# Moving the normalising and adding of most batches behind the last tiles, the last root to ScalarE, and the writes behind the last load

## The chip, the core and the metric

The kernel runs on one core of one Trainium2 chip. Its time is the device time of one execution in microseconds (us), the median of several.

## What is computed

Input x is 8 batches of 512 tokens with 128 features, float32. Two residual blocks follow one another; each adds the layer norm of its branch to x.

```
x = x + layernorm(attn(layernorm(x)))
x = x + layernorm(ffn(layernorm(x)))
attn: inp = mix*x + (1-mix)*shifted x;  h = relu(inp @ W_in.T + b_in)
      state = state*decay + h  along the sequence;  states @ W_out.T + b_out
ffn:  top-2 of 8 experts per token, softmax over the two gate logits
      y = silu(x @ w0[e]) * (x @ w1[e]) @ wo[e];  out = sum over the two of weight * y
```

The change touches only the last step: the sum of a token's two expert rows, its layer norm, and the addition to x.

## The kernel before

Everything is written out by engine, with semaphores. The 4096 tokens give 8192 (token, expert) pairs, which are sorted by expert into 71 tiles of 128 rows (TILES). After a preamble all engines walk through slots t = 0 to 75 (`slots()`). In slot t the engines work on several tiles at once: TensorE turns tile t (L1514), multiplies tile t-1 by w0 and w1 in three parts each (L1519 to L1521), turns the gated tile t-2 (L1554), and multiplies tile t-3 by wo (L1570). ScalarE takes the upper part of tile t (L586), scales the finished rows y of tile t-4 (L606, `take_y`), computes silu of t-1 (L591) and copies the turned tile t-2 (L596). VectorE computes the lower part x_lo of tile t (L1214, for which TensorE waits before the next slot) and the product silu times l2 of tile t-1 (L1221), and every fourth slot the rows' numbers and weights (L1233 to L1247). POOL sends y of tile t-4 with an indirect DMA to `pair_rows` in DRAM (L422, `send_y`).

Tiles are ordered so that the pairs of batches 0 to 5 are complete after tile 55 (FIRST_OLD_TILES = 56), those of batch 6 after tile 62 (OLD_TILES = 63) and those of batch 7 after the last. SP loads the pairs of a group of batches back to SBUF as soon as the y of those tiles have landed (`load_pairs`, L345; GROUPS are batches 0-1, 2-3, 4-5, 6 and 7). The loads of the first three groups are 1 MB each, the last two 0.5 MB.

For each batch of 4 x 128 tokens then follow, in this order: the sum of the two rows of a token (VectorE, L1252), statistics (VectorE, L1258) and their aggregate (L1264), 1/sqrt(variance + eps) by group (POOL, an add L443 and a power L447, `one_over_sd`), the offset -mean/sd by group (VectorE, L1270, `offset`), the normalising of four 128-column pieces (ScalarE, L624, `normalise4`), the addition to x (`add_normed`: POOL L454 for batches 0 and 1, VectorE L1284 for 2 to 6) and the write of the group (SP, L350, 0.5 MB for two batches). These pieces are placed by hand in the slots FIRST_OLD_TILES + 6 to + 18, behind the tile's own work of each engine, by the `if t == ...` tables of L469 to L480 (POOL), L686 to L699 (ScalarE) and L1371 to L1413 (VectorE). Since every engine works in order, a piece that waits holds up the tile work behind it.

Batch 7 comes after the slots: load, sum, statistics, aggregate, root and offset, then two of its four pieces are normalised by VectorE (L1278, L1288) and two by ScalarE (L632), added, and written with the last write. SP's queue at the end reads: load of batch 7, then the writes of groups 0 to 4, each after a wait.

Of the kernel before, what the change touches and what calls it, by code (L numbers as in the profile page):

```python
# [59 lines left out]
def sandwich_kernel(nc, x_in, w_in_in, b_in_in, w_out_in, b_out_in, decay_in, mix_in,  # L60
                    gate_in, w0_in, w1_in, wo_in, out):
    ctx = ExitStack()
    with ctx:
# [221 lines left out]
        def _(sp):  # L285
# [72 lines left out]
            load_pairs(3)  # L358
            wait_sent(TILES)
            load_pairs(4)  # L360
            sp.wait_ge(d["out"], 2)
            write_out(0)
            sp.wait_ge(d["out_end"], 2)
            write_out(1)
            sp.wait_ge(d["out_end"], 4)
            write_out(2)
            sp.wait_ge(d["out_end"], 5)
            write_out(3)
            sp.wait_ge(d["out_end"], 6)
# [4 lines left out]
        def _(pool):  # L374
# [77 lines left out]
            def add_normed(b):  # L452
                pool.wait_ge(d["normed"], b + 1)
                pool.tensor_tensor(x[:, b * G:(b + 1) * G], x[:, b * G:(b + 1) * G],  # L454
                                   half_of_pairs(b, 0), ALU.add).then_inc(d["out"], 1)

# [9 lines left out]
            for k, s, t in slots():  # L466
# [4 lines left out]
                elif t == FIRST_OLD_TILES + 11:  # L471
                    one_over_sd(1, *SD_GROUPS[1])
                elif t == FIRST_OLD_TILES + 12:
                    add_normed(0)
                elif t == FIRST_OLD_TILES + 13:
                    one_over_sd(2, *SD_GROUPS[2])
                elif t == FIRST_OLD_TILES + 14:
                    add_normed(1)
                elif t == FIRST_OLD_TILES + 16:
                    one_over_sd(3, *SD_GROUPS[3])  # L480

            one_over_sd(4, *SD_GROUPS[4])

        @block.scalar
        def _(act):
# [142 lines left out]

            def normalise_last():
# [47 lines left out]
            for k, s, t in slots():  # L677
# [8 lines left out]
                if t == FIRST_OLD_TILES + 10:  # L686
                    normalise4(0, 0, 0, G)
                elif t == FIRST_OLD_TILES + 11:
                    normalise4(0, 1, 0, G)
                elif t == FIRST_OLD_TILES + 12:  # L690
                    normalise4(1, 2, 0, G)
                elif t == FIRST_OLD_TILES + 13:
                    normalise4(1, 3, 0, G)
                elif t == FIRST_OLD_TILES + 14:
                    normalise4(2, 4, 0, G)
                elif t == FIRST_OLD_TILES + 15:
                    normalise4(2, 5, 0, G)
                elif t == FIRST_OLD_TILES + 17:
                    normalise4(3, 6, 0, G)  # L699

            normalise_last()

        @block.vector
        def _(dve):
# [576 lines left out]

            def add_normed(b):
                dve.wait_ge(d["normed"], b + 1)
                dve.tensor_tensor(x[:, b * G:(b + 1) * G], x[:, b * G:(b + 1) * G],  # L1284
                                  half_of_pairs(b, 0), ALU.add).then_inc(d["out_end"], 1)
# [75 lines left out]
            for k, s, t in slots():  # L1361
# [20 lines left out]
                elif t == FIRST_OLD_TILES + 9:  # L1382
                    aggregate(2)
                    sum_pairs(1, 3)
                    stats_of(3)
# [245 lines left out]
```

## Time and profile before

| | us |
|---|---|
| median of 3 runs (lowest, highest) | 312.19 (311.73, 312.6) |
| the profiled execution | 312.02 |
| its span (first to last instruction) | 310.2 |
| TensorE busy in the span | 253.0 (82%) |
| VectorE | 201.2 (65%) |
| ScalarE | 186.1 (60%) |
| POOL | 176.1 (57%) |

The profile is one execution. Its span leaves out 1.8 us of the execution's time. Times of rows count from the start of the span. An engine's rows may overlap by a fraction of an instruction, since the next one starts while the last elements of the one before are written; TensorE's ends are modelled. "SPq" and "POOLq" are the queues' own instructions. Matmul records are merged in rows of the timeline.

### The profile page before, as it was taken

To read this page: it belongs to the slowest core of one execution; us is meant where nothing else is said; L and a number is where in the kernel's file an instruction comes from. 1 tells how busy PE (TensorE), PEld (TensorE's weight loads), DVE (VectorE), ACT (ScalarE), POOL (GpSimd) and SP (SyncE) were. 2 spreads that over 40 slices of the span, in tenths; PEclk is the share of its full clock that TensorE was granted. 3 is DMA by queue.
4 is the path that set the end of the run, shared out by engine and by line. 5 is a ranking of instruction groups with operands and counts; after the bars stand their busy time and mean duration, and the time that the engine had idled before them with its cause. 6 is when DMAs were issued, how large, how long until landed. Compare 5 with 4: busy or idle time off the path is not lost.

```text
span 310.2 us, 6821 instructions
## 1 busy us (share of the span) xinstructions
PE 253.0 (82%) x1615; PEld 214.3 (69%) x1615; DVE 201.2 (65%) x917; ACT 186.1 (60%) x451; POOL 176.1 (57%) x197
## 2 busy tenths in 40 slices
PE   0558534469999999999999999999999999999300
PEld 0226321357988899888889888898898888878300
DVE  3787979865496568559666846785554336887512
ACT  3575455616576865856675675666666666699601
POOL 7029567267237756774874787777233333568511
PEclk9965555578999999999999999999999999999955
DMA  5999511131121122112112212432322139020056
GB/s 145 207 383 301 150 53 45 43 79 36 46 60 54 42 73 71 44 62 77 56 44 83 66 45 65 111 107 86 88 73 57 51 91 366 17 77 17 0 154 184
DMA packets 27971, 29.56 MB, mean 95 GB/s; under 512 B 4538, under 2 KB 21148, under 8 KB 27936
## 3 DMA queue, kind: packets, MB, share of 16 engines
q1 hardware_dynamic: 22672, 20.04, 22.3%
q0 software_dynamic: 4544, 8.97, 8.9%
q8 instruction: 16, 0.26, 0.4%
q10 hardware_dynamic: 720, 0.13, 0.3%
q14 instruction: 19, 0.16, 0.2%
HBM read 17.53 MB, written 12.05 MB: 95 GB/s over the span
## 4 chain that ended last, share of the span: by engine, by line
PE 70%; DVE 8%; POOL 6%; DMA 5%; ACT 4%; issue 4%; POOLq 0%; SPq 0%; DVEq 0%; ACTq 0%
PE bank L1570 18%; PE bank L1519 10%; PE bank L1520 10%; PE bank L1521 10%; PE bank L1554 9%; POOL expert_rows L411 3%; PE bank L1514 3%; PE bank L1471 2%; PE bank L1444 2%; PE bank L1455 2%; PE bank L1464 1%; DMA sb_early<-pair_rows 1%; POOL pair_rows L422 1%; DMA sb_x<-in_L_attn_x 1%; POOL sb_rs L447 1%
## 5 line engine op out<-in xcount | busy, mean ns | idle before, releaser
L422 POOL DMA_INDIRECT pair_rows<-sb_y_rows,sb_y_pair x71 | 71.2, 1003 | 59.8 <-ACT sb_y_rows L606 40.2
L411 POOL DMA_INDIRECT expert_rows<-sb_row,sb_place x64 | 63.9, 999 | 30.1 <-issue 17.6
L1570 PE MATMUL bank<-sb_w_raw,sb_gatedT 128*128 x568 | 75.0, 275 | 0.0
L1221 DVE TENSOR_TENSOR sb_w_raw<-bank,sb_w_raw 128x512 f32<-128x512 f32 x71 | 48.9, 689 | 31.5 <-PE bank L1521 20.7
L1570 PEld LDWEIGHTS bank<-sb_w_raw,sb_gatedT 128*128 128x128 f32 x568 | 69.0, 192 | 0.1
L1519 PE MATMUL bank<-sb_w_parts,sb_x_hi 128*128 x142 | 62.8, 442 | 0.3 <-DVE sb_x_lo L1214 0.3
L596 ACT ACTIVATE sb_gatedT<-bank 128x512 f32<-128x512 f32 x71 | 42.4, 597 | 32.6 <-PE bank L1554 32.4
L1520 PE MATMUL bank<-sb_w_parts,sb_x_lo 128*128 x142 | 56.7, 399 | 0.0
L1521 PE MATMUL bank<-sb_w_parts,sb_x_hi 128*128 x142 | 56.5, 398 | 0.0
L591 ACT ACTIVATE sb_w_raw<-bank 128x512 f32<-128x512 f32 x71 | 42.5, 599 | 7.4 <-PE bank L1521 6.4
L1554 PE MATMUL bank<-sb_ident,sb_w_raw 128*128 128x128 f32 x284 | 42.9, 273 | 1.1 <-DVE sb_w_raw L1221 1.1
L1214 DVE TENSOR_TENSOR sb_x_lo<-bank,sb_x_hi 128x128 fp32r<-128x128 f32 x71 | 20.4, 287 | 34.8 <-ACT sb_x_hi L586 34.4
L1554 PEld LDWEIGHTS bank<-sb_ident,sb_w_raw 128*128 128x128 f32 x284 | 34.5, 140 | 10.4 <-issue 1.3
L586 ACT ACTIVATE sb_x_hi<-bank 128x128 fp32r<-128x128 f32 x71 | 19.6, 276 | 36.4 <-PE bank L1514 36.4
L1521 PEld LDWEIGHTS bank<-sb_w_parts,sb_x_hi 128*128 128x128 f32 x142 | 27.1, 191 | 6.4
L1519 PEld LDWEIGHTS bank<-sb_w_parts,sb_x_hi 128*128 128x128 f32 x142 | 27.5, 194 | 5.1 <-issue 1.6
L1520 PEld LDWEIGHTS bank<-sb_w_parts,sb_x_lo 128*128 128x128 f32 x142 | 27.4, 193 | 3.1
L606 ACT ACTIVATE sb_y_rows<-bank,sb_y_weight 128x128 f32<-128x128 f32 x71 | 25.7, 362 | 0.3 <-PE bank L1570 0.3
L1514 PE MATMUL bank<-sb_ident,sb_taken_rows 128*128 128x128 f32 x71 | 20.1, 283 | 2.8 <-DMA sb_taken_rows<-expert_rows 2.0
L261 POOL TENSOR_TENSOR sb_w_parts<-sb_w_raw,sb_w_parts 128x512 fp32r<-128x512 f32 x8 | 10.9, 1394 | 14.1 <-ACT sb_w_parts L553 14.1
L540 ACT ACTIVATE sb_row<-sb_x,sb_nm,sb_rs 128x128 f32<-128x128 f32 x32 | 14.3, 487 | 5.2 <-DVE sb_nm L767 5.2
L1444 PE MATMUL bank<-sb_early,sb_w_inT 128*128 128x512 f32 x16 | 12.0, 845 | 4.6 <-DVE sb_early L804 4.6
(177 smaller groups left out, 348.5 us busy)
## 6 DMA issues: line engine op xcount, KB each, us to landing
sb_taken_rows<-expert_rows SPq DMA_DIRECT2D x71, 65.5 KB, 1.8
sb_w_raw<-in_L_ffn_w SPq DMA_DIRECT2D x2, 2048.0 KB, 14.1
sb_w_raw<-pair_rows SPq DMA_DIRECT2D x3, 1024.0 KB, 7.2
out_dram<-sb_x SPq DMA_DIRECT2D x3, 512.0 KB, 6.2
pair_rows<-sb_y_rows,sb_y_pair POOLq DMA_INDIRECT x71, 2.5
sb_x<-in_L_attn_x SPq DMA_DIRECT2D x4, 256.0 KB, 6.4
expert_rows<-sb_row,sb_place POOLq DMA_INDIRECT x64, 2.3
sb_early<-pair_rows SPq DMA_DIRECT2D x2, 512.0 KB, 3.8
```

What stands on the lines that cost most here:

```text
L411: pool.indirect_dma_start(expert_rows[:, :], bass.IndirectOffsetOnAxis(ap=place[b % ROWS][:, k, j:j + 1], axis=0), row[b % ROWS][:, j, :], ...
L422: pool.indirect_dma_start(pair_rows[:, :], bass.IndirectOffsetOnAxis(ap=y_pair[group % 2][:, t % PAIRS:t % PAIRS + 1], axis=0), y_rows[slo ...
L591: act.activation(silu[t % 2][:], p_l1[:], ACT.Silu).then_inc(c["silu"], 1)
L596: act.activation(gatedT[t % 2][:], p_gatedT[:], ACT.Copy).then_inc(c["gatedT"], 1)
L606: act.activation(y_rows[t % Y_SLOTS][:], p_y[t % 2][:, 0:D], ACT.Copy, scale=y_weight[group % 2][:, t % PAIRS:t % PAIRS + 1]).then_inc(c[" ...
L1221: dve.tensor_tensor(gated[t % 2][:], p_l2[:], silu[t % 2][:], ALU.mult).then_inc(c["gated"], 1)
L1514: pe.transpose(p_xeT[:, 0:P], taken_rows[:, t % RING, 0:D], ident[:]).then_inc(c["xeT_ps"], 1)
L1519: pe.matmul(to, x_hi, w_hi, start=True, stop=False)
L1520: pe.matmul(to, x_lo, w_hi, start=False, stop=False)
L1521: return pe.matmul(to, x_hi, w_lo, start=False, stop=True)
L1554: last = pe.transpose(p_gatedT[:, n * P:(n + 1) * P], gated[t % 2][:, n * P:(n + 1) * P], ident[:])
L1570: last = pe.matmul(p_y[t % 2][:, 0:D], gatedT[t % 2][:, n * P:(n + 1) * P], wo.rearrange("p o d -> p (o d)"), start=(n == 0), stop=(n == F ...
```

## The change

ScalarE's normalisations in the slots become two pieces a slot instead of four, begin one slot later, and cover batches 0 and 1 and half of batch 2; the other half of batch 2, and batches 3 and 4, follow after the last slot. VectorE takes over the normalising of batches 5 and 6, after the slots. POOL's two additions go to VectorE (slots 71 and 72), and all other additions come after the slots. Three of the offsets move behind the product of a later slot. POOL's power for batch 6 comes after its last send. For batch 7 the root is ScalarE's, with the reciprocal on VectorE, in place of POOL's add and power; ScalarE loads the table of the root ahead of it. SP writes group 0 ahead of the last load, and groups 3, 1 and 2 only when the last load has landed.

```diff
--- before.py
+++ after.py
@@ -356,17 +356,18 @@
                 load_pairs(g)
             wait_sent(OLD_TILES)
             load_pairs(3)
+            sp.wait_ge(d["out"], 2)
+            write_out(0)
             wait_sent(TILES)
             load_pairs(4)
-            sp.wait_ge(d["out"], 2)
-            write_out(0)
-            sp.wait_ge(d["out_end"], 2)
+            sp.wait_ge(s_pairs_in[4], 16)
+            sp.wait_ge(d["out"], 5)
+            write_out(3)
+            sp.wait_ge(d["out"], 6)
             write_out(1)
-            sp.wait_ge(d["out_end"], 4)
+            sp.wait_ge(d["out"], 7)
             write_out(2)
-            sp.wait_ge(d["out_end"], 5)
-            write_out(3)
-            sp.wait_ge(d["out_end"], 6)
+            sp.wait_ge(d["out_end"], 1)
             write_out(4)
             sp.wait_ge(s_out, 16 * len(GROUPS))
 
@@ -449,11 +450,6 @@
                     minus_half[:].broadcast_to([P, (end - first) * G]),
                     ALU.pow).then_inc(d["rs"], 1)
 
-            def add_normed(b):
-                pool.wait_ge(d["normed"], b + 1)
-                pool.tensor_tensor(x[:, b * G:(b + 1) * G], x[:, b * G:(b + 1) * G],
-                                   half_of_pairs(b, 0), ALU.add).then_inc(d["out"], 1)
-
             for n in range(W_SPLITS // 2):
                 pool.wait_ge(s_w_hi, n + 1)
                 first, size = w_split(n)
@@ -470,16 +466,10 @@
                     one_over_sd(0, *SD_GROUPS[0])
                 elif t == FIRST_OLD_TILES + 11:
                     one_over_sd(1, *SD_GROUPS[1])
-                elif t == FIRST_OLD_TILES + 12:
-                    add_normed(0)
                 elif t == FIRST_OLD_TILES + 13:
                     one_over_sd(2, *SD_GROUPS[2])
-                elif t == FIRST_OLD_TILES + 14:
-                    add_normed(1)
-                elif t == FIRST_OLD_TILES + 16:
-                    one_over_sd(3, *SD_GROUPS[3])
-
-            one_over_sd(4, *SD_GROUPS[4])
+
+            one_over_sd(3, *SD_GROUPS[3])
 
         @block.scalar
         def _(act):
@@ -625,6 +615,12 @@
                                           scale=rs4[:, n:n + 1], bias=nm4[:, n:n + 1])
                 if end == G:
                     last.then_inc(d["normed"], 1)
+
+            def root_last():
+                last = slice((B - 1) * G, B * G)
+                act.wait_ge(d["mv"], B)
+                act.activation(sd4[:, last], mv4[:, last, 1], ACT.Sqrt,
+                               bias=eps[:]).then_inc(d["sd"], 1)
 
             def normalise_last():
                 act.wait_ge(d["nm"], len(SD_GROUPS))
@@ -683,21 +679,22 @@
                 a_slot(k, s, 1)
                 gated_turned(t - 2)
                 a_slot(k, s, 2)
-                if t == FIRST_OLD_TILES + 10:
-                    normalise4(0, 0, 0, G)
-                elif t == FIRST_OLD_TILES + 11:
-                    normalise4(0, 1, 0, G)
+                if t == FIRST_OLD_TILES + 11:
+                    normalise4(0, 0, 0, 2)
                 elif t == FIRST_OLD_TILES + 12:
-                    normalise4(1, 2, 0, G)
+                    normalise4(0, 0, 2, G)
                 elif t == FIRST_OLD_TILES + 13:
-                    normalise4(1, 3, 0, G)
+                    normalise4(0, 1, 0, 2)
                 elif t == FIRST_OLD_TILES + 14:
-                    normalise4(2, 4, 0, G)
+                    normalise4(0, 1, 2, G)
                 elif t == FIRST_OLD_TILES + 15:
-                    normalise4(2, 5, 0, G)
-                elif t == FIRST_OLD_TILES + 17:
-                    normalise4(3, 6, 0, G)
-
+                    normalise4(1, 2, 0, 2)
+
+            normalise4(1, 2, 2, G)
+            normalise4(1, 3, 0, G)
+            normalise4(2, 4, 0, G)
+            act.activation(unused[:], eps[:], ACT.Sqrt)
+            root_last()
             normalise_last()
 
         @block.vector
@@ -1279,10 +1276,22 @@
                                              ALU.mult, ALU.add)
                 last.then_inc(d["normed_here"], 1)
 
+            def one_over_last():
+                last = slice((B - 1) * G, B * G)
+                dve.wait_ge(d["sd"], len(SD_GROUPS))
+                dve.reciprocal(rs4[:, last], sd4[:, last]).then_inc(d["rs"], 1)
+
+            def add(b):
+                dve.tensor_tensor(x[:, b * G:(b + 1) * G], x[:, b * G:(b + 1) * G],
+                                  half_of_pairs(b, 0), ALU.add).then_inc(d["out"], 1)
+
             def add_normed(b):
                 dve.wait_ge(d["normed"], b + 1)
-                dve.tensor_tensor(x[:, b * G:(b + 1) * G], x[:, b * G:(b + 1) * G],
-                                  half_of_pairs(b, 0), ALU.add).then_inc(d["out_end"], 1)
+                add(b)
+
+            def add_here(b):
+                dve.wait_ge(d["normed_here"], b - 4)
+                add(b)
 
             def add_last(j):
                 return dve.tensor_tensor(
@@ -1383,8 +1392,8 @@
                     aggregate(2)
                     sum_pairs(1, 3)
                     stats_of(3)
+                elif t == FIRST_OLD_TILES + 10:
                     offset(0)
-                elif t == FIRST_OLD_TILES + 10:
                     aggregate(3)
                     sum_pairs(2, 4)
                     stats_of(4)
@@ -1392,32 +1401,35 @@
                     aggregate(4)
                     sum_pairs(2, 5)
                     stats_of(5)
+                elif t == FIRST_OLD_TILES + 12:
                     offset(1)
-                elif t == FIRST_OLD_TILES + 12:
                     aggregate(5)
                 elif t == FIRST_OLD_TILES + 13:
                     sum_pairs(3, 6)
                     stats_of(6)
+                elif t == FIRST_OLD_TILES + 14:
                     offset(2)
-                elif t == FIRST_OLD_TILES + 14:
                     aggregate(6)
-                    add_normed(2)
                 elif t == FIRST_OLD_TILES + 15:
-                    add_normed(3)
+                    add_normed(0)
                 elif t == FIRST_OLD_TILES + 16:
-                    add_normed(4)
-                    offset(3)
-                elif t == FIRST_OLD_TILES + 17:
-                    add_normed(5)
-                elif t == FIRST_OLD_TILES + 18:
-                    add_normed(6)
-
+                    add_normed(1)
+
+            normalise4(2, 5, 0, G)
+            add_here(5)
+            add_normed(2)
+            offset(3)
+            normalise4(3, 6, 0, G)
+            add_here(6)
+            add_normed(3)
+            add_normed(4)
             sum_pairs(4, 7)
             stats_of(7)
             aggregate(7)
+            one_over_last()
             offset(4)
             normalise4(4, 7, G // 2, G)
-            dve.wait_ge(d["normed_here"], 1)
+            dve.wait_ge(d["normed_here"], 3)
             add_last(G // 2)
             dve.wait_ge(d["normed_end"], 1)
             add_last(0).then_inc(d["out_end"], 1)
```

ScalarE, from the last slots to its end. L591/L581 is silu, L596/L586 the copy of the turned tile, L606/L596 the taking of y, L624/L614 the normalising; the second number is the line in the changed kernel. Before:

```order
L624 ACTIVATE sb_w_raw<-sb_w_raw,sb_nm,sb_rs 128x128 x4
L606 ACTIVATE sb_y_rows<-bank,sb_y_weight 128x128
L591 ACTIVATE sb_w_raw<-bank 128x512
L596 ACTIVATE sb_gatedT<-bank 128x512
L624 ACTIVATE sb_w_raw<-sb_w_raw,sb_nm,sb_rs 128x128 x4
L606 ACTIVATE sb_y_rows<-bank,sb_y_weight 128x128
L596 ACTIVATE sb_gatedT<-bank 128x512
L606 ACTIVATE sb_y_rows<-bank,sb_y_weight 128x128
L624 ACTIVATE sb_early<-sb_early,sb_nm,sb_rs 128x128 x4
L606 ACTIVATE sb_y_rows<-bank,sb_y_weight 128x128
L632 ACTIVATE sb_early<-sb_early,sb_nm,sb_rs 128x128 x2
```

Batch 6 (`sb_early`, x4) is normalised between the last two takings of y.

The same place of ScalarE in the changed kernel:

```order
L614 ACTIVATE sb_w_raw<-sb_w_raw,sb_nm,sb_rs 128x128 x2
L596 ACTIVATE sb_y_rows<-bank,sb_y_weight 128x128
L581 ACTIVATE sb_w_raw<-bank 128x512
L586 ACTIVATE sb_gatedT<-bank 128x512
L614 ACTIVATE sb_w_raw<-sb_w_raw,sb_nm,sb_rs 128x128 x2
L596 ACTIVATE sb_y_rows<-bank,sb_y_weight 128x128
L586 ACTIVATE sb_gatedT<-bank 128x512
L596 ACTIVATE sb_y_rows<-bank,sb_y_weight 128x128 x2
L614 ACTIVATE sb_w_raw<-sb_w_raw,sb_nm,sb_rs 128x128 x10
L696 ACT_TABLE_LOAD
L622 ACTIVATE sb_sd<-sb_mv,sb_eps 128x4
L628 ACTIVATE sb_early<-sb_early,sb_nm,sb_rs 128x128 x2
```

No normalising stands ahead of the last three takings of y; ten pieces, the table load and the root come behind them. (The activation that only calls for the table, after the load, is left out here.)

VectorE, from the last tile's product (L1218, L1221 before) to the last sum (L1249) in the changed kernel. L1285 is an addition to x, L1275 a normalisation, L1267 the offset:

```order
L1218 TENSOR_TENSOR sb_w_raw<-bank,sb_w_raw 128x512
L1285 TENSOR_TENSOR sb_x<-sb_x,sb_w_raw 128x512 x2
L1275 TENSOR_SCALAR sb_w_raw<-sb_w_raw,sb_rs,sb_nm 128x128 x4
L1285 TENSOR_TENSOR sb_x<-sb_x,sb_w_raw 128x512 x2
L1267 SCALAR_TENSOR_TENSOR sb_nm<-sb_mv,sb_rs 128x4
L1275 TENSOR_SCALAR sb_early<-sb_early,sb_rs,sb_nm 128x128 x4
L1285 TENSOR_TENSOR sb_x<-sb_x,sb_early 128x512
L1285 TENSOR_TENSOR sb_x<-sb_x,sb_w_raw 128x512 x2
L1249 TENSOR_TENSOR sb_early<-sb_early 128x4x128
```

Before, one addition stood ahead of that product and four behind it, and one offset; now seven additions, eight normalisations and one offset stand between product and sum.

SP's end, as a difference (- before, + changed):

```order
-L345 DMA sb_early<-pair_rows 128x1024 x2
-L350 DMA out_dram<-sb_x 128x8x128 x3
-L350 DMA out_dram<-sb_x 128x4x128 x2
+L345 DMA sb_early<-pair_rows 128x1024
+L350 DMA out_dram<-sb_x 128x8x128
+L345 DMA sb_early<-pair_rows 128x1024
+L350 DMA out_dram<-sb_x 128x4x128
+L350 DMA out_dram<-sb_x 128x8x128 x2
+L350 DMA out_dram<-sb_x 128x4x128
```

The write of group 0 moved between the two last loads, and the write of group 3 ahead of those of groups 1 and 2.

## Rows read from the trace of the kernel before

**Rows 1.** The page, section 4: engines' shares of the chain that ended last.
```profile
PE 70%; DVE 8%; POOL 6%; DMA 5%; ACT 4%; issue 4%; POOLq 0%; SPq 0%; DVEq 0%; ACTq 0%
```

**Rows 2.** Busy time by stretch: length; PE, PEld, DVE, ACT, POOL; clock; DMA share; GB/s.
```profile
290.00:294.00 4.00, 0.94 (x8) 0.75 (x7) 0.86 (x3) 2.07 (x6) 3.41 (x4) 1.00 0.01 0
```

**Rows 3.** The chain that ended last, by time: start, length, what.
```profile
294.98 2.11 DMA pair_rows<-sb_y_rows,sb_y_pair
...
297.21 4.00 DMA sb_early<-pair_rows
...
303.34 0.20 POOL sb_sd L443
```

**Rows 4.** Timeline of ScalarE (start, length), at the start and the end.
```profile
3.19 1.28 ACT L493 ACT_TABLE_LOAD   x1 [3.19 <-issue]
...
5.99 0.30 ACT L497 ACTIVATE sb_sd<-sb_mv,sb_eps 128x4 f32<-128x4 f32 x1 [1.30 <-DVE sb_mv L754]
6.73 1.65 ACT L514 ACTIVATE sb_early<-sb_x,sb_nm,sb_rs 128x128 f32<-128x128 f32 x4 [0.44 <-DVE sb_nm L767]
...
293.78 0.35 ACT L606 ACTIVATE sb_y_rows<-bank,sb_y_weight 128x128 f32<-128x128 f32 x1
```

**Rows 5.** Timeline of TensorE, slots 67 to 73.
```profile
271.49 0.27 PE L1514 MATMUL bank<-sb_ident,sb_taken_rows 128*128 128x128 f32 x1
...
274.35 0.27 PE L1514 MATMUL bank<-sb_ident,sb_taken_rows 128*128 128x128 f32 x1
...
278.09 0.33 PE L1514 MATMUL bank<-sb_ident,sb_taken_rows 128*128 128x128 f32 x1 [0.73 <-DVE sb_x_lo L1214]
...
281.05 0.27 PE L1514 MATMUL bank<-sb_ident,sb_taken_rows 128*128 128x128 f32 x1
...
284.32 0.49 PE L1519 MATMUL bank<-sb_w_parts,sb_x_hi 128*128 x1 [0.26 <-DVE sb_x_lo L1214]
...
286.24 1.06 PE L1570 MATMUL bank<-sb_w_raw,sb_gatedT 128*128 x8
288.35 0.66 PE L1554 MATMUL bank<-sb_ident,sb_w_raw 128*128 128x128 f32 x4 [1.05 <-DVE sb_w_raw L1221]
288.84 2.10 PE L1570 MATMUL bank<-sb_w_raw,sb_gatedT 128*128 x16
```

**Rows 6.** Timeline of VectorE, slot 68 to the end.
```profile
277.67 0.17 DVE L1270 SCALAR_TENSOR_TENSOR sb_nm<-sb_mv,sb_rs 128x8 f32<-128x8 f32 x1 [0.66 <-POOL sb_rs L447]
...
283.80 0.17 DVE L1270 SCALAR_TENSOR_TENSOR sb_nm<-sb_mv,sb_rs 128x8 f32<-128x8 f32 x1 [1.15 <-POOL sb_rs L447]
...
284.69 1.68 DVE L1233 TENSOR_TENSOR sb_not_first<-sb_taken_rows,sb_tile_expert 128x3 f32<-128x3 f32 x1
...
287.61 0.68 DVE L1221 TENSOR_TENSOR sb_w_raw<-bank,sb_w_raw 128x512 f32<-128x512 f32 x1
...
292.11 0.69 DVE L1284 TENSOR_TENSOR sb_x<-sb_x,sb_w_raw 128x512 f32<-128x512 f32 x1
...
304.89 0.60 DVE L1278 TENSOR_SCALAR sb_early<-sb_early,sb_rs,sb_nm 128x128 f32<-128x128 f32 x2
```

**Rows 7.** Timeline of POOL: a send of the start, then slots 68 to 74.
```profile
38.27 0.97 POOL L411 DMA_INDIRECT expert_rows<-sb_row,sb_place  x1 [0.30 <-issue]
...
275.49 2.14 POOL L447 TENSOR_TENSOR sb_rs<-sb_sd,sb_minus_half 128x8 f32<-128x8 f32 x1
...
285.03 1.30 POOL L454 TENSOR_TENSOR sb_x<-sb_x,sb_w_raw 128x512 f32<-128x512 f32 x1
...
292.20 1.51 POOL L422 DMA_INDIRECT pair_rows<-sb_y_rows,sb_y_pair  x1 [0.20 <-issue]
```

**Rows 8.** From issue to landing: all five of L345, then all five of L350.
```profile
DMA to landing us min/median/max: 3.6/4.9/9.3
...
DMA to landing us min/median/max: 2.3/5.2/7.1
```

**Rows 9.** Busy time by stretch, as in rows 2: one us with writes only.
```profile
304.00:305.00 1.00, 0.00 (x0) 0.00 (x0) 0.28 (x2) 0.12 (x1) 0.66 (x1) 0.50 1.15 348
```

## The prediction

> **What bounds the kernel now.** The page comes first: TensorE has 70% of the chain that ended last [rows 1], but the change leaves every matmul where it was, so the question is how the span ends. The table by stretch says where that end begins: from 290 to 294 TensorE is busy for 0.94 of 4 us and no engine is full [rows 2]. The chain of waits shows what the end is made of [rows 3]: POOL sends the last rows of y from 294.98, 2.11 us; the last pairs load from 297.21, 4.00 us; then sum, statistics, aggregate, POOL's add (303.34) and power, offset, normalisation, add and the last write. ScalarE's timeline shows that the last y was taken late: L606 at 293.78 [rows 4], though TensorE's last matmuls (288.84, 2.10 us) had ended at 290.94 [rows 5]. Ahead of it in ScalarE's order stood the normalising of batch 6, which waited for VectorE's offset and that for POOL's power. The timeline of TensorE gives a second loss: a tile's slot is 2.86 us long from 271.49 to 274.35, but the next ones begin at 278.09, 281.05 and, without its transpose, 284.32; the last tile's turn waits until 288.35 [rows 5]. The causes stand on VectorE: offset(1) at 277.67 and offset(2) at 283.80, each with an x_lo behind it and each after a wait for POOL, and the product L1221 of the last tile at 287.61, behind a three-element L1233 that took 1.68 us and an add [rows 6].
>
> **TensorE.** The offsets move behind the product of their slot, POOL's two adds go, and ScalarE has two normalisations a slot instead of four. What can be won, against a slot of 2.84: 3.74 - 2.84 = 0.90 in slot 68; 2.96 - 2.84 = 0.12 in slot 69; 3.27 - 2.76 (the next slot begins without its L1514) = 0.51 in slot 70; and the 1.05 us that the last turn waited. Sum 2.6 us [rows 5]. Is the room there? VectorE was idle for 0.66 us ahead of offset(1), so its work of slot 67 was done at 277.01, and TensorE wants x_lo(68) at 274.35 + 2.84 = 277.2: it fits, since that work is the same and starts no later. offset(1) then waits for POOL's power (it ended at 275.49 + 2.14 = 277.63) with only an aggregate behind it [rows 6, 7]. ScalarE's four normalisations take 1.65 us, two 0.83 [rows 4]. So TensorE's end goes from 290.94 to 288.3, and the last y is taken at 288.35.
>
> **The last y.** From L606's start to POOL's were 1.20 us (293.78 to 294.98), which would give 289.55. But the sends now come close together. The last layer of tile 68 (L1570, 286.24) moves by 0.90 + 0.12 + 0.51 to 284.7 and ends 1.06 later, ScalarE's two normalisations end at about 286.1, so y(68) is taken at 286.2 and sent at 287.4; back to back a send takes 0.97 and 0.30 of gap [rows 7], so the next are at 288.7 and 290.0. POOL's rate is what counts: **290.0 instead of 294.98, -5.0**. Its power for batch 6 now stands behind the sends.
>
> **POOL against VectorE.** A send that began 0.09 us after an add of VectorE (292.11) took 1.51 instead of 0.97 us, and the L1233 of 1.68 us ended as POOL's add L454 did, 286.33 [rows 6, 7]. So an operation of VectorE with two inputs in SBUF and a POOL instruction that reads SBUF exclude each other. In the change VectorE runs two adds, four tensor_scalar and one more add (some 3.2 us) beside the sends of tiles 68 to 70. I take **+0.2** in all, since VectorE must then stop for ScalarE's batch 2; bounds 0 and 3 x 0.54 = 1.6. The Trainium skill, SBUF — State Buffer, section Who interferes with whom, says that tensor_tensor with both inputs in SBUF contends with GpSimd's reads, but that tensor_tensor, unlike tensor_copy, was not seen to stall a DMA. By it the adds would cost the sends 0 where I took +0.2; the 1.51 us speaks against it.
>
> **The last load.** It had four writes behind it in SP's queue and took 4.00; the minimum of L345, 3.6, is the load of batch 6, with none [rows 3, 8]. write_out(0) now goes ahead, at about 287; with the median landing of L350, 5.2 us [rows 8], it is through at 292.2, as the load is issued. I take **-0.4**; bounds 0 and -0.4. SP's new wait for two adds stands ahead of this load; the second add is at about 286.5, 5 us before the load could go.
>
> **Work ahead of the last sum.** The load lands at 290.2 + 2.11 + 0.12 + 3.6 = 296.0. ScalarE: ten normalisations of 0.41 from 288.7 [rows 4]: 292.8. VectorE: POOL's last send ends at 291.2, its add and power take 1.35 (303.34 to 304.89 less the offset) [rows 3, 6]: 292.6; offset 0.2; four tensor_scalar 1.2; three adds at 0.62 to 0.69, 2.0: 296.0 [rows 6]. So this chain and the load are even; bounds 0 and +0.7, taken 0. ScalarE's table load was 1.28 us [rows 4], so it is ready at 294.3, and the root is wanted at 298.1.
>
> **The last root.** From POOL's L443 at 303.34 to VectorE's normalisation at 304.89 were 1.55 us [rows 3, 6]. The step by ScalarE's root and VectorE's reciprocal is in the trace at the start: L497 at 5.99, L514 at 6.73, 0.74 us [rows 4]. **-0.8.**
>
> **The last write.** Writes 3, 1 and 2 (1.31 MB) start when the load lands; at the 348 GB/s of a stretch with writes only [rows 9] they need 3.8 us, and with 1 us to the first bytes are through at 300.8. The last normalisations started 3.65 us after the landing (301.24 to 304.89), now 2.85; with the 1.4 to the last add as before its write is issued at 300.3, and its own bytes need the same 1 us to start. So 0; bounds 0 and +0.6.
>
> **Sum.** -5.0 + 0.2 - 0.4 - 0.8 = -6.0. The span of 310.2 becomes 304.2, the profiled execution's 312.02 becomes 306.0; the median of the runs, 312.19, is 0.17 above that execution: **306.1 us**. 0.3% (0.9 us) is about what a measurement of this kernel can tell from no change.
>
> **Rivals.**
> (1) VectorE takes the place of the removed waits. Behind offset(3) stand four normalisations and three adds, and then the last sum. For: no cover by the sum above, and port losses delay POOL's power too. Against: ScalarE's part is done 3 us earlier. Price +0.5 to +1.5: about 307.1. Chance 0.2.
> (2) TensorE keeps stalls: the two normalisations still delay x_hi, or the offset still meets a late power. For: that power took 2.14 us and starts no earlier [rows 7]. Against: nothing that TensorE needs in that slot stands behind it. Price up to 2.6, with 1.9 of them 308.0. Chance 0.11.
> (3) POOL is locked out for longer: each of three sends loses 0.54. Price +1.4: 307.5. Chance 0.07. The Trainium skill, same page and section, has a rule for this: tensor_scalar can enter a two-port mode, and GpSimd then fully blocks. No row of before has a send beside one.
> (4) Slower than before: SP stands at its new wait with the last load behind it. Place: VectorE's add of batch 1 in slot 72, itself behind ScalarE's second half of that batch in slot 70. Each us that it comes after 292.4 is a us of the end. At 297.6 to 299.4 the gain of 6.1 is gone to within 0.9; from 299.4 it is slower: 313.1. For: the wait is new and on the chain's own queue. Against: the add would have to be 13 us late. Chance 0.02 for slower, 0.02 for no change.
>
> **Numbers.** The forecast has 0.58, from 305.0 (the +0.2 doesn't come, and the last y is sent 1.20 us after L606 rather than at POOL's rate: 0.65) to 306.9. The range reaches over (1), (3) and half of (2): 305.0 to 307.9. Faster 0.96, same 0.02, slower 0.02.
>
> **What would show it.** TensorE's L1514 go on at 2.84 us to the last tile and its last matmul ends near 288.3. The last y is taken near 288.35. POOL's last send starts near 290, 1.27 after the one before; a length over 1.1 is the port. The load is issued at 292.4 and lands 3.6 later with no write in its queue. The last sum waits for the load: if the profile names no DMA ahead of it, (1) is right. From aggregate to normalisation 0.8 instead of 1.6. Wrong altogether: a slot over 3.2 us after 276, or a last load issued after 294.

## The result and the profile after

The changed kernel takes 305.04 us (median of 6 runs, 303.22 to 306.17) against 311.89 (6 runs of before): ratio 0.9772, 95% interval 0.9749 to 0.9795. My 306.1 against 312.19 was a ratio of 0.9805, just outside that interval. The ratio times the new median of before is 304.8, 0.2 us below my range; the bare median stands on the range's lower end. The direction and nearly every step held. One term was missing.

The profiled execution took 305.05, its span is 303.3: 6.9 us less than before, where I had 6.0. TensorE's timeline (start, then length; lines of the changed kernel: L1526 turns a tile, L1566 the gated tile, L1582 is the product with wo):

```profile
274.24 0.27 PE L1526 MATMUL bank<-sb_ident,sb_taken_rows 128*128 128x128 f32 x1
...
277.07 0.27 PE L1526 MATMUL bank<-sb_ident,sb_taken_rows 128*128 128x128 f32 x1
...
279.92 0.27 PE L1526 MATMUL bank<-sb_ident,sb_taken_rows 128*128 128x128 f32 x1
...
285.99 2.20 PE L1582 MATMUL bank<-sb_w_raw,sb_gatedT 128*128 x16
```

Against [rows 5]: the slots go on at 2.83 to 2.85 us, no row of TensorE waits, and the last matmuls end at 288.19 instead of 290.94. The page of the changed kernel has TensorE at 9 tenths in every slice from the eleventh on until it stops:

```profile
PE   0666542568999999999999999999999999999900
```

POOL's timeline from tile 67's send to its end:

```profile
284.53 0.98 POOL L423 DMA_INDIRECT pair_rows<-sb_y_rows,sb_y_pair  x1 [1.31 <-ACT sb_y_rows L596]
287.25 0.98 POOL L423 DMA_INDIRECT pair_rows<-sb_y_rows,sb_y_pair  x1 [1.74 <-ACT sb_y_rows L596]
288.53 0.98 POOL L423 DMA_INDIRECT pair_rows<-sb_y_rows,sb_y_pair  x1 [0.31 <-issue]
289.82 1.12 POOL L423 DMA_INDIRECT pair_rows<-sb_y_rows,sb_y_pair  x1 [0.30 <-issue]
290.93 0.24 POOL L444 TENSOR_TENSOR sb_sd<-sb_mv,sb_eps 128x4 f32<-128x4 f32 x1
291.25 1.04 POOL L448 TENSOR_TENSOR sb_rs<-sb_sd,sb_minus_half 128x4 f32<-128x4 f32 x1
```

The last three sends are 1.28 us apart, at POOL's own rate ("issue", not a wait for ScalarE), and the last starts at 289.82 instead of 294.98 [rows 3]. The chain that ended last, from there:

```profile
289.82 2.25 DMA pair_rows<-sb_y_rows,sb_y_pair
...
292.19 3.67 DMA sb_early<-pair_rows
...
295.88 0.70 DVE sb_early L1249
...
297.93 0.31 ACT sb_sd L622
...
298.26 0.19 DVE sb_rs L1282
...
298.47 0.17 DVE sb_nm L1267
...
298.67 0.61 DVE sb_early L1275 x2
```

The load lands 3.67 us after its issue (4.00 in [rows 3]); from the root to the normalisation are 0.74 us. VectorE was done just ahead of the load:

```profile
294.28 1.29 DVE L1285 TENSOR_TENSOR sb_x<-sb_x,sb_w_raw 128x512 f32<-128x512 f32 x2
295.88 0.69 DVE L1249 TENSOR_TENSOR sb_early<-sb_early 128x512 f32<-128x512 f32 x1 [0.31 <-DMA sb_early<-pair_rows]
```

It waited 0.31 us for the DMA, so the two chains into the last sum are as even as the forecast had them.

What I had not looked at stands in the rows of line L63, with which every queue closes. A DRAIN is the closing instruction of one queue, SP's COMPARE_BRANCH ends its wait for the last write, and the EVENT_SEMAPHORE is each queue's signal that it is done. Of the kernel before (smallest, median and largest duration in ns, then first and last start):

```profile
L63 POOLq EVENT_SEMAPHORE  x2: 17/17/17, 310.0 to 310.1; - x2
...
L63 POOLq DRAIN  x1: 6402/6402/6402, 303.6 to 303.6; - x1
L63 ACTq DRAIN  x1: 906/906/906, 304.9 to 304.9; - x1
L63 DVEq DRAIN  x1: 528/528/528, 305.8 to 305.8; - x1
L63 SPq COMPARE_BRANCH  x1: 45/45/45, 308.6 to 308.6; - x1
L63 SPq DRAIN  x1: 7/7/7, 308.8 to 308.8; - x1
```

and of the changed kernel:

```profile
L63 POOLq DRAIN  x1: 6403/6403/6403, 291.2 to 291.2; - x1
...
L63 SPq COMPARE_BRANCH  x1: 45/45/45, 302.9 to 302.9; - x1
L63 SPq DRAIN  x1: 7/7/7, 303.1 to 303.1; - x1
```

Before, SP had seen the last write land and was done at 308.8, and the program ended at 310.2, when POOL's queue had closed (303.6 + 6.4 = 310.0). So the last write was not what set the end. In the changed kernel POOL's queue closes at 297.6 and SP ends the program. The waits of SP's queue say the same, first before, then after:

```profile
SPq L63 <- PEq L63: 1.4, 1, 1.4
```

```profile
SPq L63 <- PEq L63: 0.2, 1, 0.2
```

(The view names TensorE's queue, but by the rows above ScalarE's and VectorE's had closed by 306.4 and TensorE's long before; only POOL's was still open.) A second row went the other way: the last write was issued at 306.31 and SP went on at 308.6, 2.3 us; now at 300.1 and 302.9, 2.8 us.

### The profile page after: what moved, and what is told of

Read it like the earlier page. It is cut to its first block, busy times and chain, and to the rows that moved or that the text cites. A ratio compares the mean times of both kernels' runs of the same rounds, so it can differ in the third digit from the quotient of the medians.

```text
span 303.3 us, 6824 instructions
## 1 busy us (share of the span) xinstructions
PE 252.2 (83%) x1615; PEld 214.7 (71%) x1615; DVE 203.2 (67%) x928; ACT 185.4 (61%) x446; POOL 171.3 (56%) x193
## 4 chain that ended last, share of the span: by engine, by line
PE 76%; DVE 8%; DMA 5%; POOL 4%; issue 3%; ACT 3%; SPq 0%; DVEq 0%; POOLq 0%; ACTq 0%
PE bank L1582 20%; PE bank L1531 11%; PE bank L1533 11%; PE bank L1532 11%; PE bank L1566 10%; POOL expert_rows L412 3%; PE bank L1526 3%; PE bank L1483 3%; PE bank L1467 2%; PE bank L1456 2%; PE bank L1476 1%; DMA sb_x<-in_L_attn_x 1%; DMA sb_early<-pair_rows 1%; PE bank L1448 1%; DVE sb_early L809 1%
## 5 line engine op out<-in xcount | busy, mean ns | idle before, releaser
L1582 PE MATMUL bank<-sb_w_raw,sb_gatedT 128*128 x568 | 75.1, 275 | 0.0
L1218 DVE TENSOR_TENSOR sb_w_raw<-bank,sb_w_raw 128x512 f32<-128x512 f32 x71 | 49.0, 690 | 33.4 <-PE bank L1533 23.0
L1582 PEld LDWEIGHTS bank<-sb_w_raw,sb_gatedT 128*128 128x128 f32 x568 | 69.0, 192 | 0.2 <-issue 0.2
L586 ACT ACTIVATE sb_gatedT<-bank 128x512 f32<-128x512 f32 x71 | 42.4, 596 | 34.6 <-PE bank L1566 34.5
L581 ACT ACTIVATE sb_w_raw<-bank 128x512 f32<-128x512 f32 x71 | 42.6, 600 | 7.3 <-PE bank L1533 6.3
L1566 PE MATMUL bank<-sb_ident,sb_w_raw 128*128 128x128 f32 x284 | 42.8, 273 | 0.0
L1566 PEld LDWEIGHTS bank<-sb_ident,sb_w_raw 128*128 128x128 f32 x284 | 34.6, 140 | 8.8 <-issue 0.7
L596 ACT ACTIVATE sb_y_rows<-bank,sb_y_weight 128x128 f32<-128x128 f32 x71 | 25.8, 363 | 1.0 <-PE bank L1582 1.0
L1526 PE MATMUL bank<-sb_ident,sb_taken_rows 128*128 128x128 f32 x71 | 20.0, 282 | 2.0 <-DMA sb_taken_rows<-expert_rows 2.0
```

Of the source, the lines that this page charges most:

```text
L581: act.activation(silu[t % 2][:], p_l1[:], ACT.Silu).then_inc(c["silu"], 1)
L586: act.activation(gatedT[t % 2][:], p_gatedT[:], ACT.Copy).then_inc(c["gatedT"], 1)
L596: act.activation(y_rows[t % Y_SLOTS][:], p_y[t % 2][:, 0:D], ACT.Copy, scale=y_weight[group % 2][:, t % PAIRS:t % PAIRS + 1]).then_inc(c[" ...
L1218: dve.tensor_tensor(gated[t % 2][:], p_l2[:], silu[t % 2][:], ALU.mult).then_inc(c["gated"], 1)
L1526: pe.transpose(p_xeT[:, 0:P], taken_rows[:, t % RING, 0:D], ident[:]).then_inc(c["xeT_ps"], 1)
L1566: last = pe.transpose(p_gatedT[:, n * P:(n + 1) * P], gated[t % 2][:, n * P:(n + 1) * P], ident[:])
```

## The experiments

The theory: five parts of the end moved as forecast, and two more things act at the end. One is POOL's closing (theory A in the first three runs), the other that the last write queues behind the writes ahead of it. The rival: only the chain through the last write counts.

The profiled executions differ by up to 3 us before any of the changed code runs: slot 60 of TensorE began at 251.64 before, 251.56 in the changed kernel, and from 249.79 to 252.93 in the others. The table and the text therefore give the end as the span less the start of slot 60 of the same profile. In the six profiles with the same code up to the last send, that send starts 38.26 to 38.28 us after slot 60; the load behind it lands in 3.43 to 3.70 us. So a step of 0.2 us or less is not told apart from the load's own variation. The medians, with a spread of some 1 to 3 us, resolve the larger steps alone.

| kernel | median us | ratio to before (95%) | span | slot 60 | span less slot 60 |
|---|---|---|---|---|---|
| before | 311.89 | | 310.2 | 251.64 | 58.56 |
| changed | 305.04 | 0.9772 (0.9749, 0.9795) | 303.3 | 251.56 | 51.74 |
| changed, again | 304.83 | 0.9748 (0.9714, 0.9781) | 303.5 | 251.82 | 51.68 |

**The last root back on POOL**, in the changed kernel.

```diff
             one_over_sd(3, *SD_GROUPS[3])
+            one_over_sd(4, *SD_GROUPS[4])
...
-            act.activation(unused[:], eps[:], ACT.Sqrt)
-            root_last()
...
-            one_over_last()
```

> The changed kernel with the last root back on POOL (its add and power), everything else as changed. Theory A (the end waits for POOL's queue, whose closing DRAIN row lasts 6.40 us from its last power in both profiles): the power starts near 298.25, its drain ends near 304.65, span about 304.9, 1.6 us over the changed kernel's 303.3. Theory B (only the chain through the last write sets the end): 0.8 us over, the length of the step, so 304.1. Steps up to the last aggregate as in the changed kernel under both.

Measured: 306.08 us, ratio 0.9822 (0.9771 to 0.9874); span 304.6 with slot 60 at 251.53, so 53.07, 1.33 us over the changed kernel. Its load happened to land 0.24 us sooner (3.43), so the step costs 1.57 with an equal load, as theory A has it. POOL's closing:

```profile
L63 POOLq DRAIN  x1: 6367/6367/6367, 298.0 to 298.0; - x1
...
L63 SPq DRAIN  x1: 7/7/7, 303.8 to 303.8; - x1
```

SP was done at 303.8; the end was POOL's 298.0 + 6.37 = 304.4.

**The last root alone moved**, in the kernel before: the same lines added there, and POOL's `one_over_sd(4, ...)` removed.

> The kernel before with the last root alone moved to ScalarE and VectorE. Theory A (POOL's drain held the end of before at 310.0 while SP was done at 308.8): the drain now starts near 291 and is off the end; the chain gives 0.8 and the end 1.2 to 1.4 less whatever the last write loses behind the others, so a span near 308.5, 1.7 us less. Theory B (chain only): 0.8 us less, 309.4.

Measured: 310.06 us, ratio 0.9946 (0.9916 to 0.9976); span 308.5, slot 60 at 251.90: 56.60, **1.96 less than before**. The last add to x ends 53.86 after slot 60 instead of 54.64, so 0.8 of it is the chain's; the other 1.2 is the closing. Theory A. This is the part of the change whose worth I had as 0.8.

**One small POOL instruction that nobody waits for**, in the changed kernel, at the last aggregate.

```diff
             one_over_sd(3, *SD_GROUPS[3])
+            pool.wait_ge(d["mv"], B)
+            pool.tensor_tensor(pool_tail[:], mv4[:, (B - 1) * G:B * G, 1],
+                               eps[:].broadcast_to([P, G]), ALU.add)
```

> The changed kernel with one small POOL add (128x4, into a tile that nothing reads) that waits for the last aggregate. Nothing waits for it. Theory A (a drain of 6.40 us follows POOL's last instruction): the add starts near 298.0, the end is near 304.6, 1.3 us over. Theory B: no change from the changed kernel, 303.3, within 0.2.

Measured: 305.07 us; span 303.8, slot 60 at 251.74: 52.06, 0.32 over. That is neither theory A's 1.3 nor theory B's 0 to 0.2. The rows say why:

```profile
298.07 0.20 POOL L475 TENSOR_TENSOR sb_pool_tail<-sb_mv,sb_eps 128x4 f32<-128x4 f32 x1 [5.57 <-DVE sb_mv L1265]
```

```profile
L63 POOLq DRAIN  x1: 5545/5545/5545, 298.0 to 298.0; - x1
...
L63 SPq DRAIN  x1: 7/7/7, 303.2 to 303.2; - x1
```

The closing is not always 6.40 us long: it began at 298.0 as with the root on POOL, but lasted 5.55. What is constant is the time from the end of POOL's last instruction: 298.27 to 303.55 = 5.28 here, 304.66 to 310.0 = 5.3 before, 299.00 to 304.37 = 5.4 with the root on POOL. The longer row holds the 1.04 us of the power, too. So theory A as I had written it is refuted; what fits all three is "5.3 us behind the end of the last instruction", a form made after the fact and so in need of a run of its own.

**The small instruction behind the last add** was to try that form: the same lines in the changed kernel, with `pool.wait_ge(d["out_end"], 1)`.

> The changed kernel with the one small POOL add (into a tile that nothing reads) moved to wait for the last add to x, 300.07. Theory A (POOL's queue closes 5.3 us after the end of its last instruction, as 5.28 to 5.37 in five profiles): end at 300.4 + 5.3 + 0.2 = 305.9, 2.6 us over the changed kernel, with SP done 2.7 earlier. Theory B (a closing of fixed length 6.4 from its start): 306.8. No effect: 303.3.

Measured: 308.9 us, ratio 0.9873 (0.9836 to 0.9909); span 307.3, slot 60 at 252.93: 54.37, 2.63 over the changed kernel. Forecast 2.6. SP was done at 304.5, POOL's queue 2.5 us later. An instruction of 0.20 us whose result nobody reads costs 2.6 us, by its place alone:

```profile
301.58 0.20 POOL L475 TENSOR_TENSOR sb_pool_tail<-sb_mv,sb_eps 128x4 f32<-128x4 f32 x1 [7.89 <-DVE sb_x L1301]
```

```profile
L63 POOLq DRAIN  x1: 5547/5547/5547, 301.5 to 301.5; - x1
...
L63 SPq DRAIN  x1: 7/7/7, 304.5 to 304.5; - x1
```

**The writes not behind the last load**, in the changed kernel.

```diff
-            sp.wait_ge(s_pairs_in[4], 16)
             sp.wait_ge(d["out"], 5)
             write_out(3)
```

> The changed kernel without SP's wait for the last load ahead of the writes of groups 3, 1 and 2: they go as soon as their adds are done (294.3, 294.9, 295.6), behind the load in the same queue. If the write queue is what made the last write take 2.8 us instead of 2.3: landing back at 2.3, span 302.8, 0.5 less. If the wait is what made the load shorter (3.67 against 4.00): the load lands 0.2 to 0.3 later and the net is 0 to 0.3 less.

Measured: 304.25 us, ratio 0.9765 (0.9716 to 0.9814); span 301.7, slot 60 at 250.49: 51.21, 0.53 less than the changed kernel. The load landed 3.62 us after its issue (3.67 with the wait), so the wait did nothing for it: the writes, free to go as soon as their adds are done, are issued from 293.33 on, 2.2 us behind the load, where the kernel before issues them 0.4 us behind it. The last write took 2.3 us again, from 298.97 to 301.3, since the writes ahead of it were issued 1.5 us earlier, counted from slot 60. The 0.5 is theirs, and the wait is a small loss.

**The writes behind the last load**, in the kernel before.

```diff
             load_pairs(4)
+            sp.wait_ge(s_pairs_in[4], 16)
             sp.wait_ge(d["out"], 2)
             write_out(0)
```

> The kernel before with one wait added: SP issues the writes only when the last load has landed. The load should land 3.6 instead of 4.0 us after its issue (theory A, the writes in the queue cost it 0.4); if it stays at 4.0, the load's length has another cause (theory B). The end is set by POOL's queue, 5.3 us behind the end of POOL's last power, so it moves with the load: span 309.8 by A, 310.2 by B; the last write now queues behind 1.8 MB and lands 2.3 to 3.0 us after its issue without showing in the end.

Measured: 311.74 us, ratio 0.9979 (0.9956 to 1.0002); span 310.5, slot 60 at 252.09: 58.41, 0.15 less. The load landed in 3.56 instead of 4.00, as theory A has it; in the four profiles in which the first write was issued 0.4 us behind the load it took 4.00 to 4.06, in the ten others 3.43 to 3.70. But the last write, behind 1.8 MB, took 3.8 us (issued 306.3, SP on at 310.1), more than the 3.0 I allowed. SP was done 0.3 us after POOL's queue and ended the program, so the gain of the load did not reach the end. What helps the load here is paid by the last write; the change avoids it by writing group 0 early.

**Batch 6 normalised behind the last taking of y**, in the kernel before.

```diff
-                elif t == FIRST_OLD_TILES + 17:
-                    normalise4(3, 6, 0, G)
...
+            normalise4(3, 6, 0, G)
             normalise_last()
```

> The kernel before with the normalising of batch 6 behind the last taking of y on ScalarE, and nothing else. Theory A (POOL's rate counts): y of tile 70 is taken at 291.0 instead of 293.8, but POOL sends tile 69 only at 292.2, behind its own power for batch 6, so tile 70 goes at about 293.8: 1.2 us less at the end. Theory B (what I wrote of ScalarE's order alone): 2.8 less.

Measured: 311.13 us, ratio 0.9991 (0.9958 to 1.0024); span 307.9, slot 60 at 249.79: 58.11, 0.45 less. Nearer to theory A's 1.2 than to theory B's 2.8, and less than both, since the two last sends were lengthened by VectorE's adds:

```profile
290.36 1.51 POOL L422 DMA_INDIRECT pair_rows<-sb_y_rows,sb_y_pair  x1 [0.20 <-issue]
292.18 1.43 POOL L422 DMA_INDIRECT pair_rows<-sb_y_rows,sb_y_pair  x1 [0.30 <-issue]
```

```profile
290.27 0.68 DVE L1283 TENSOR_TENSOR sb_x<-sb_x,sb_w_raw 128x512 f32<-128x512 f32 x1
292.07 0.69 DVE L1283 TENSOR_TENSOR sb_x<-sb_x,sb_early 128x512 f32<-128x512 f32 x1 [1.11 <-ACT sb_early L624]
```

Each send began 0.1 us into a two-input add and ended 0.85 to 0.92 us after it.

**And POOL's power for batch 6 behind its last send**: that edit, and

```diff
-                elif t == FIRST_OLD_TILES + 16:
-                    one_over_sd(3, *SD_GROUPS[3])
...
+            one_over_sd(3, *SD_GROUPS[3])
             one_over_sd(4, *SD_GROUPS[4])
```

> As the run with batch 6 normalised late, and POOL's power for batch 6 behind its last send. The sends of tiles 68 to 70 then follow at 1.28 us from 289.7: tile 70 at 292.2, 2.7 us less than before at the end, span 307.5. If the sends aren't at POOL's rate, tile 70 goes 1.2 us after its y is taken, which gives the same 292.2; the starts of tiles 69 and 70 tell it.

Measured: 309.31 us, ratio 0.9911 (0.9891 to 0.9931); span 307.4, slot 60 at 251.39: 56.01, 2.55 less than before. Sends at 289.42, 290.88 and 292.15, 0.97 us each. With both edits the end gains 2.1 us on what ScalarE's order alone gave (0.45). About half of the 2.1 is the power's own place; the other half, 1.0 us, is that the last two sends take 0.97 instead of 1.51 and 1.43, because VectorE's adds now come after them.

**All of the change in the slots but ScalarE's share**: that kernel, with POOL's two adds on VectorE behind the slots and the three offsets where the change has them. ScalarE still normalises batches 0 to 5, four pieces a slot.

> As the run before it, and POOL's two adds on VectorE behind the slots, and the three offsets one slot later. What is left out of the change in the slots is then only that ScalarE does two normalisations a slot and not four. Theory A (four a slot make ScalarE the bound, its slot being about 3.0 us): TensorE's slots from 68 on are 2.9 to 3.0 us long, tile 68's y is taken at about 287.9, tile 70 sent at 291.6. Theory B (only the offsets and POOL's adds stalled TensorE): slots of 2.84, tile 70 sent at 290.0, as in the changed kernel.

Measured: 310.75 us, ratio 0.9946 (0.9924 to 0.9969); span 306.7, slot 60 at 249.83: 56.87, which is 0.86 *more* than without these two edits, though still 1.69 less than before. The slots are those of theory A (2.93 and 2.96 us for tiles 68 and 69), and then comes a stall that I had not forecast. ScalarE's and VectorE's rows show it:

```profile
283.23 1.65 ACT L619 ACTIVATE sb_w_raw<-sb_w_raw,sb_nm,sb_rs 128x128 f32<-128x128 f32 x4 [1.08 <-DVE sb_nm L1264]
284.79 0.35 ACT L601 ACTIVATE sb_y_rows<-bank,sb_y_weight 128x128 f32<-128x128 f32 x1
285.04 0.58 ACT L586 ACTIVATE sb_w_raw<-bank 128x512 f32<-128x512 f32 x1
```

```profile
285.65 0.69 DVE L1215 TENSOR_TENSOR sb_w_raw<-bank,sb_w_raw 128x512 f32<-128x512 f32 x1 [1.78 <-ACT sb_w_raw L586]
```

The offset now comes later than ScalarE wants it: it waits 1.08 us, silu of the last tile stands behind it, VectorE waits 1.78 us for silu, and TensorE 1.49. So removing one engine's stall had only moved it to the next. Not all of the 0.86 comes from there. The last add to x ends 52.53 after slot 60, against 52.06 in the run before: 0.47. The other 0.4 is the last write's. SP's first write waits for the adds of batches 0 and 1, which now come after the slots, so the last write stands behind 1.8 MB as in the run with the writes behind the load, and takes 3.9 us; SP and not POOL ends this program:

```profile
L63 POOLq DRAIN  x1: 6368/6368/6368, 299.7 to 299.7; - x1
...
L63 SPq COMPARE_BRANCH  x1: 45/45/45, 306.3 to 306.3; - x1
```

 The slots free of stalls come with ScalarE's new share (two pieces a slot, beginning one slot later, with VectorE taking batches 5 and 6): between this kernel and the changed one the issue of the last load moves 3.1 us (293.54 - 249.83 against 292.19 - 251.56). How much of that is the halving and how much the later beginning was not tried apart.

**tensor_scalar beside the sends**, in the changed kernel.

```diff
             add_here(5)
+            for n in range(8):
+                dve.tensor_scalar(port_probe[:, n, :], sums(5 * G + n % G), ..., ALU.mult, ALU.add)
```

> The changed kernel with eight more tensor_scalar of 128x128 on VectorE (into a tile that nothing reads), behind the add of batch 5, so that they run beside the sends of tiles 69 and 70. Theory A (tensor_scalar holds the port as the two-input adds do): the two sends take 1.1 to 1.3 us instead of 0.98, and the end is 0.2 to 0.5 later. Theory B (it doesn't, as with the one that overlapped the send at 287.25 by 0.1): 0.98 both, and the end as before, since VectorE then still waits for POOL's power.

Measured, a single execution: 306.04 us, span 304.3, slot 60 at 252.76: 51.54, 0.20 less than the changed kernel. Theory B:

```profile
289.18 2.14 DVE L1422 TENSOR_SCALAR sb_port_probe<-sb_w_raw,sb_rs,sb_nm 128x128 f32<-128x128 f32 x8
```

```profile
289.74 0.98 POOL L424 DMA_INDIRECT pair_rows<-sb_y_rows,sb_y_pair  x1 [0.30 <-issue]
291.02 1.00 POOL L424 DMA_INDIRECT pair_rows<-sb_y_rows,sb_y_pair  x1 [0.31 <-issue]
```

The two sends that begin in this run of tensor_scalar keep their length, within 0.02 us. In the changed kernel the send of 1.12 us had begun during the add of batch 2 (289.39 to 290.08); here that add came after its start.

**A better version**: the changed kernel without SP's wait, and with slot 71's two normalisations behind the last y. These two pieces stand directly ahead of the taking of tile 68's y in the changed kernel (285.28 to 286.15), so only the last two takings there are free of normalising, not the last three.

```diff
-            sp.wait_ge(s_pairs_in[4], 16)
...
-                elif t == FIRST_OLD_TILES + 15:
-                    normalise4(1, 2, 0, 2)
...
-            normalise4(1, 2, 2, G)
+            normalise4(1, 2, 0, G)
```

> The changed kernel itself, on the chip of the three runs beside it, as what they are compared with: span 303.3, plus or minus 1 us for the part before tile 4, which varies from one execution to the next.

> The changed kernel without SP's wait for the last load, and with ScalarE's two normalisations of slot 71 (first half of batch 2) behind the last taking of y. Tile 68's y is then taken 0.4 earlier (285.65 instead of 286.05), the sends of 68 to 70 follow at POOL's rate, and the end is 0.4 earlier, on top of the 0.5 of the last write: 0.9 us below the changed kernel. Rival: VectorE, whose add of batch 2 now waits 0.8 longer for ScalarE, is behind the load, and the 0.4 is lost: 0.5 below.

Measured on one chip: 303.21 us (302.32 to 304.94) against the changed kernel's 304.83 (303.22 to 306.0); ratios to before 0.9709 (0.9674 to 0.9743) and 0.9748. Span 301.5, slot 60 at 250.74: 50.76, against 51.68 for the changed kernel beside it and 51.74 in the first profile, so 0.9 to 1.0 less, as forecast. Of it 0.5 is the last write, and 0.4 the issue of the load: the last send starts 0.23 earlier, and it takes 0.98 instead of 1.12, since the add of batch 2 now comes after its start. The medians differ by 1.6 and their runs overlap; the profiles carry the claim. VectorE's wait for the load is down to 0.16 us:

```profile
294.55 0.69 DVE L1246 TENSOR_TENSOR sb_early<-sb_early 128x512 f32<-128x512 f32 x1 [0.16 <-DMA sb_early<-pair_rows]
```

## Why the prediction was right and where it failed

- **TensorE** (end at 288.3): 288.19. Right, with slots of 2.84. Where I put the stalls down to the offsets and POOL's adds, I had only a part of the cause: the run without ScalarE's new share shows that those two edits alone gain nothing at the end.
- **The last y** (taken 288.35, sends at 287.4, 288.7, 290.0): 288.23, and 287.25, 288.53, 289.82. That POOL's order and rate count more than ScalarE's order is shown by the two runs on batch 6, 0.45 us against 2.55; I had read the stretch in which POOL was busy for 3.41 of 4.00 us as one where no engine is full [rows 2].
- **POOL against VectorE** (+0.2): the last send took 1.12 instead of 0.98 and its landing 2.25 instead of 2.11, +0.14. The mechanism holds for two-input adds; the two sends beside tensor_scalar show none of it, so rival (3) falls. (Its "No row of before has a send beside one" is not so: the send at 286.76 began in the last 0.08 us of the three-element tensor_scalar L1247, and took 0.99.) The Trainium skill's sentence in SBUF — State Buffer, Who interferes with whom, that tensor_tensor was not seen to stall a DMA, is not what these rows show (1.51, 1.43 and 1.12 us).
- **The last load** (-0.4): 3.67 against 4.00, -0.33. The cause I gave was partly off: free of writes is what counts, but it came from write 0 being ahead and the other adds being later than the load's issue. The new wait gained nothing.
- **Work ahead of the last sum** (even with the load, 0 taken): VectorE was done 0.31 us before the load landed. Right.
- **The last root** (-0.8): from the landing to the last add 4.21 us instead of 5.06, -0.85.
- **The last write** (0, bounds 0 and +0.6): +0.5 for the landing, within the bounds, and **-1.2 that no bound held**. This is the step of the prediction that failed. I wrote that "its write is issued at 300.3, and its own bytes need the same 1 us to start. So 0", and took for granted that the landing of that write ended the program before as well. But the kernel before ended 1.4 us after SP was done, with POOL's queue. Moving the root off POOL was therefore worth 0.8 on the chain and 1.2 at the end; alone in the kernel before it gave 1.96.

The sum then reads: last load's issue -5.0, load -0.3, landing to last add -0.85, last write +0.5, closing -1.2: -6.9. The forecast had -6.0. Of the 0.9 between them the closing is 1.2, and without the last write's +0.5, which went the other way, the forecast would have missed by more: that much of its nearness is luck. The rest is the +0.2 for the port, which left the load's issue at -5.0 and not -4.8.

The range's lower end was also set worse than it looks. The better values that I gave for 305.0 are worth 0.65 and reach only 305.45; the last 0.45 had no term behind it, and none stood for what I had not seen.

Of the rivals, (1) came within 0.31 us, (2) and (4) did not show (no slot over 2.85 us; the last load was issued at 292.19, with SP's new wait long met), and (3) was tried and fell.

## What to carry to other kernels

Before costing the end of a kernel, look at which engine's queue closes last, not at which instruction is last: here POOL's needed 5.3 us after its last instruction. An instruction on it that ends less than 5.3 us before the other queues are done therefore delays the end by what is missing, even if nobody reads its result (0.3 us in one place, 2.6 in another). Where a chain passes through an in-order engine that sends at a fixed rate, first take other work out from between the sends, and what lengthens them (2.1 us here); making its input ready earlier gave little until then. Edits that each remove a stall need not add up: two of them made the end of this kernel later, in part through the last write, until the third engine's share was cut.

## What the runs showed of the hardware that I had not expected

- POOL's queue closes 5.3 us after the end of its last instruction, in all fourteen profiles (the rows of the kernel before and of the runs made for it give 5.28 to 5.37, with a start known to 0.1), whether that is a power of 1.04 us or an add of 0.20. When the last instruction was a send, as in the run with the root alone moved, the same held (296.23 to 301.5). VectorE's closing row was 0.53 us, ScalarE's 0.91. Why POOL's takes so long, and whether it would in a kernel without indirect DMAs, was not tried.
- POOL's instruction for an indirect DMA that starts during a VectorE add of two SBUF operands is lengthened by most of what is left of the add: 1.51 instead of 0.97 us with 0.60 left, 1.12 with 0.27 left. The two that started during tensor_scalar of 128x128 were not (0.98 and 1.00). An add that starts after the send did not lengthen it either (0.98 at 287.25, with an add from 287.37).
- The same code before slot 60 took from 249.8 to 252.9 us in the profiles; nearly all of the difference is there when TensorE turns tile 4. Its cause was not looked for.
